# Layer 2's experts: results scattered to token order as they come, in place of a gather at the end

## The chip, the cores and the metric

One NeuronCore of a Trainium2 chip runs the whole program: TensorE (matmuls; the trace calls it PE, and PEld its weight loads), VectorE (DVE), ScalarE (ACT), GpSimd (POOL) and SyncE (SP, which issues plain DMAs). The metric is the time of one execution on the device in microseconds; less is better. The time of a kernel is the median of several runs.

## The reference

The program is a chain of four layers, each a mixer and a feed-forward part on 4096 tokens of 128 numbers. The change touches the feed-forward part of layer 2 alone, a mixture of eight experts with one expert per token and a capacity:

```python
def _route(tokens, router_w):
    capacity = int(math.ceil(T / E * CAPACITY_FACTOR))      # T 4096, E 8: 640
    probs = jax.nn.softmax(tokens @ router_w.T, axis=-1)
    top1_idx = jnp.argmax(probs, axis=-1)
    top1_prob = jnp.max(probs, axis=-1)
    order = jnp.lexsort((-top1_prob, top1_idx))
...
    pos_in_group = jnp.arange(T) - start[sorted_e]
    keep = jnp.zeros((T,), bool).at[order].set(pos_in_group < capacity)
    return jnp.where(keep, top1_idx, 0).astype(jnp.int32)

final_e = _route(tokens, router_w)
for e in range(E):
    h = jax.nn.relu(tokens @ W1[e] + b1[e])
    y = h @ W2[e] + b2[e]
    out = out + jnp.where((final_e == e)[:, None], y, 0.0)
```

`tokens` is the layer norm of the running state `x`, and `out` is added to `x`. A token that finds its expert full goes to expert 0.

## The kernel before

A token is one row of 128 numbers. In SBUF token `i * 128 + p` lies on partition `p` as tile `i` (32 tiles, `X` the state, `XN` its norm, `XT` the norm turned so that the features lie on the partitions). Layer 2's experts are `moe_capacity`, in three pieces, each a stage or a block with a barrier of all engines at its end (lines 60 to 64, and the block's own).

The first is a block of its own in which POOL clears `zero` (line 2010). The next is `capacity_route`: norm, turning, logits, softmax, and then the rank of each token inside its expert, found with 32 rounds of comparisons on VectorE and counting matmuls. In it ScalarE copies the turned groups out (`norm.take`, line 125) and then waits for VectorE's shifted logits, of which it takes the exponential (line 1921). SP loads the weights and writes seven blocks of zeros to DRAM in `prefetch`. Its result is `idx`, for each token the row of a DRAM tensor: rows 0 to 4479 are seven buckets of 640 rows for experts 1 to 7, and rows from 4480 on are the 4096 tokens in order, for those of expert 0.

In the last stage, `experts`, the work is cut into 22 units. Units 0 to 7 (the direct units) are expert 0 applied to all tokens from `XT`, 512 each, needing no routing. Units 8 to 21 are experts 1 to 7 in two parts each, 3 tiles and 2 tiles of 128 rows. A unit runs over TensorE (up, down, and turning back), ScalarE (ReLU and bias) and VectorE, which copies the result from PSUM to one of four buffers `yo` (line 2149). The order is written out by hand for each engine.

DMAs around it: POOL scatters the 32 tiles of `XN` to `xs_dram` by `idx`, one indirect DMA a tile (line 2033), beside the direct units. SP stores each unit's `yo` to `ys_dram` (line 2051) and loads the buckets of experts 1 to 7 (line 2045), the first two after unit 6's store. When all 22 stores have landed, POOL gathers from `ys_dram` by `idx`, again one indirect DMA a tile (line 2038), and VectorE adds the rows to `X`, a group of four tiles at a time (line 2162).

## Time and profile before

| | us |
|---|---|
| median of 3 runs | 3671.94 (3671.51 to 3673.9) |
| the profiled execution, time on the device | 3670.11 |
| the profiled execution, span from first to last instruction | 3668.4 |
| stretch that the change touches, clearing to last addition | 2150.8 to 2517.4 |
| of it: direct units | about 2296 to 2380 |
| of it: experts 1 to 7 | about 2380 to 2473 |
| of it: gathers and additions | about 2473 to 2517 |

A row of the timeline gives the start in us from the span's start, the time in us, the engine, the line of the kernel, the operation, what it writes and reads, and in square brackets how long the engine had been idle and what ended that. A row of the groups gives the count behind an x, then the busy time in us and the mean in ns. DMA-issuing instructions don't count as busy on SP, but the indirect ones on POOL do. "experts_", "route_" and "cap_" ahead of a name are the stage it belongs to.

### The profile page before, as it was taken

The numbers are of one execution on the slowest core, as the hardware profiler recorded it, in microseconds if no ns is written. First come the engines' busy times: TensorE is split into PE (matmuls) and PEld (weight loads), VectorE is DVE, ScalarE is ACT, GpSimd is POOL, SyncE is SP. The second block draws the span as 40 slices with busy tenths as digits, with TensorE's granted clock in tenths as the row PEclk, the third lists the DMA queues.
The fourth block names the chain that finished last, engine by engine and source line by source line (L and its number), as shares of the span: only waits on it lengthen the run. The fifth ranks groups of instructions, "written<-read, shape, count | busy, mean of one in ns | idle before, by whom it ended". The sixth has DMA issues, their size and how long they took to land. (4 is left out here: it accounts for less than half of the span.)

```text
span 3668.4 us, 31380 instructions
## 1 busy us (share of the span) xinstructions
PE 2677.9 (73%) x8896; PEld 1455.9 (40%) x8904; DVE 2129.6 (58%) x3695; ACT 1420.2 (39%) x3926; POOL 951.0 (26%) x620
## 2 busy tenths in 40 slices
PE   2007888999999889999877766782687787377317
PEld 1003344555555544444344442351344443255303
DVE  7997531222222366565534458013999996678686
ACT  1004333111111156666543320231798898233003
POOL 0003565000000000000122210303899999000005
PEclk6558999999999989999878879896887787689557
DMA  2001112000000074545200020112000000000001
GB/s 51 0 0 47 47 48 62 0 0 0 0 0 0 13 148 139 147 138 143 74 1 1 1 72 1 50 46 69 1 1 1 1 1 1 23 1 1 2 0 29
DMA packets 106429, 124.40 MB, mean 34 GB/s; under 512 B 21771, under 2 KB 59788, under 8 KB 106028
## 3 DMA queue, kind: packets, MB, share of 16 engines
q1 hardware_dynamic: 104236, 118.56, 12.2%
q0 software_dynamic: 2048, 4.20, 0.4%
q8 instruction: 55, 0.90, 0.1%
q14 instruction: 90, 0.74, 0.1%
HBM read 108.55 MB, written 14.16 MB: 33 GB/s over the span
## 5 line engine op out<-in xcount | busy, mean ns | idle before, releaser
L2325 POOL TENSOR_TENSOR dots_pr<-dots_g 128x1536 f32<-128x1536 f32 (+3 forms) x118 | 356.5, 3063 | 66.6 <-DVE dots_g L2450 54.0
L1012 DVE SCALAR_TENSOR_TENSOR attn_sim<-attn_sc,attn_mask 128x512 f32<-128x512 f32 (+3 forms) x256 | 125.8, 491 | 316.9 <-PE attn_sc L938 313.8
L938 PE MATMUL attn_sc<-attn_q,attn_xb 128*128 128x512 f32 (+3 forms) x768 | 295.0, 486 | 0.0
L949 PE MATMUL attn_op<-attn_sim,attn_v 128*128 128x512 f32 (+3 forms) x768 | 295.0, 486 | 0.0
L1298 DVE TENSOR_TENSOR grp_h<-grp_sq,grp_cb 128x512 f32<-128x512 f32 x256 | 176.5, 692 | 191.9 <-ACT grp_sq L1186 171.8
L1126 PE MATMUL grp_po<-grp_h,grp_down 128*128 128x512 f32 x512 | 266.4, 602 | 5.7 <-DVE grp_h L1298 5.7
L1118 PE MATMUL grp_ph<-all_xt,grp_up 128*128 128x512 f32 x512 | 264.0, 598 | 0.5 <-ACT grp_sg L1202 0.5
L2338 PE MATMUL dots_pu<-delta_wE,all_xt 128*128 128x264 f32 x512 | 193.3, 524 | 97.0 <-DVE dots_g L2450 95.6
L1180 ACT ACTIVATE grp_r<-grp_ph 128x512 f32<-128x512 f32 x272 | 162.4, 597 | 185.6 <-PE grp_ph L1118 183.9
L626 POOL TENSOR_TENSOR mix_h<-mix_r,mix_cb 128x512 f32<-128x512 f32 x128 | 179.4, 1413 | 123.8 <-ACT mix_r L540 90.3
L2392 ACT ACTIVATE dots_pr<-dots_pr 128x128 f32<-128x128 f32 x704 | 206.2, 300 | 3.5 <-POOL dots_pr L2325 3.5
L938 PEld LDWEIGHTS attn_sc<-attn_q,attn_xb 128*128 128x128 f32 x768 | 141.0, 190 | 125.7 <-issue 107.1
L2338 PEld LDWEIGHTS dots_pu<-delta_wE,all_xt 128*128 128x128 f32 x512 | 118.6, 249 | 175.8 <-DVE dots_g L2450 148.9
L2325 POOL TENSOR_TENSOR all_xn<-dots_g 128x1536 f32<-128x1536 f32 (+3 forms) x58 | 180.1, 3137 | 3.3 <-PE dots_fold L2348 3.3
L949 PEld LDWEIGHTS attn_op<-attn_sim,attn_v 128*128 128x128 f32 x768 | 141.0, 190 | 98.4 <-issue 68.9
L2447 DVE TENSOR_TENSOR dots_m<-dots_pu,dots_sg 128x512 f32<-128x512 f32 x256 | 164.7, 685 | 24.7 <-ACT dots_sg L2373 14.4
L2348 PE MATMUL dots_fold<-dots_pr,all_ident 128*128 128x512 f32 x336 | 160.0, 632 | 25.3 <-ACT dots_pr L2379 25.3
L378 PE MATMUL mix_po<-mix_woT,mix_y 128*128 128x128 f32 x128 | 17.1, 298 | 213.7 <-DVE mix_y L738 213.7
L2450 DVE SCALAR_TENSOR_TENSOR dots_g<-dots_m,dots_pu 128x512 f32<-128x512 f32 x256 | 163.3, 679 | 0.0
L1186 ACT ACTIVATE grp_sq<-grp_r 128x512 f32<-128x512 f32 x256 | 159.1, 621 | 0.0
L987 ACT ACTIVATE attn_sim<-attn_sc 128x512 f32<-128x512 f32 x128 | 76.4, 597 | 205.6 <-PE attn_sc L938 205.6
L1126 PEld LDWEIGHTS grp_po<-grp_h,grp_down 128*128 128x128 f32 x512 | 94.4, 191 | 138.8 <-issue 95.9
(612 smaller groups left out, 5341.5 us busy)
## 6 DMA issues: line engine op xcount, KB each, us to landing
grp_cb<-grp_combine SPq DMA_DIRECT2D x512, 128.0 KB, 3.2
mix_cb<-top_weights SPq DMA_DIRECT2D x64, 256.0 KB, 3.2
cap_xs<-cap_zero SPq DMA_DIRECT2D x7, 320.0 KB, 4.6
experts_xe<-cap_xs SPq DMA_DIRECT2D x7, 320.0 KB, 3.3
all_x<-in_L_attn_x_dram SPq DMA_DIRECT2D x4, 512.0 KB, 5.4
cap_w<-in_L_ffn_W_dram SPq DMA_DIRECT2D x1, 2048.0 KB
cap_ys<-experts_yo SPq DMA_DIRECT2D x8, 256.0 KB, 2.3
delta_h<-all_xn SPq DMA_DIRECT2D x1, 2048.0 KB
```

Of the source, the lines that this page charges most:

```text
L626: nc.gpsimd.tensor_tensor(h[:, J % HB], r[:, J % RB], cb[:, n % CB], ALU.mult).then_inc(h_ready, 1)
L938: nc.tensor.matmul(sc[k % SC][:, 0:w], xb[:, m * P:(m + 1) * P], q[:, par, n0:n0 + w], start=True, stop=True).then_inc(s_mm, 1)
L949: ins = nc.tensor.matmul(op[half][:, n0 - half * GROUP:n0 - half * GROUP + w], v[:, par, m], sim[:, par, k, 0:w], start=False, stop=False)
L1118: nc.tensor.matmul(ph[J % 2][:], w, XT[:, g * GROUP:(g + 1) * GROUP], start=True, stop=True).then_inc(up_mm, 1)
L1126: nc.tensor.matmul(po[g % 2][:], w, h[:, J % HB], start=(j == 0), stop=(j == NJ - 1)).then_inc(down_mm, 1)
L1180: nc.scalar.activation(r[:, J % RB], ph[J % 2][:], ACT.Relu).then_inc(relu_done, 1)
L1298: tt(h[:, J % HB], sq[:, J % RB], cb[:, n % CB], ALU.mult).then_inc(h_done, 1)
L2325: nc.gpsimd.tensor_tensor(dst, a, key, ALU.mult).then_inc(pp_ready, 1)
L2338: ins = nc.tensor.matmul(heads(n % PB)[:, q * HQ:(q + 1) * HQ], XTj[:, k // 2, j], wE[:, 1 - k % 2, h0:h0 + HQ], start=True, stop=True)
L2392: ins = nc.scalar.activation(v_, v_, ACT.Relu, accum_out=dots[:, 8 + r, j, h0:h0 + 1])
L2447: tt(m[:, sh], x[..., sh + 1:sh + 1 + D_], sg[:, n % PB], ALU.mult).then_inc(m_ready, 1)
L2450: ins = stt(g[:, I % 2, k, :, sh * D_:(sh + 1) * D_], m[:, sh], 0.0, x[..., 0:D_], ALU.max, ALU.mult)
```

## The change

Each row that is scattered to a bucket now carries a 129th number, the number of its token. The tile `rows` holds the norm's 128 numbers, copied by ScalarE, and the number, written by VectorE. Bucket rows which no token takes are filled beforehand with zeros and with numbers from 4096 up, so that they name rows behind the tokens. The direct units store their results to `y_dram` in token order. From each bucket VectorE takes the numbers (`place`), and POOL scatters each unit's results of experts 1 to 7 to the token's row of `y_dram`, one indirect DMA a tile (35 in all), as the results come. At the end SP loads `y_dram` in eight plain DMAs.

```diff
@@ capacity_route
@@ scalar
                 for g in range(NG):
                     norm.take(act, g)
+                act.wait_ge(norm.xn_ready, NT)
+                for g in range(NG):
+                    nc.scalar.activation(rows[:, g * TPG:(g + 1) * TPG, 0:C], XN[:, g * TPG:(g + 1) * TPG], ACT.Copy).then_inc(rows_ready, 1)
                 act.wait_ge(shifted, 1)
                 nc.scalar.activation(ex[:], lg[:], ACT.Exp).then_inc(exp_ready, 1)
...
@@ vector
                 dve.wait_ge(made, 3 + E)
+                c.link(nc.vector.tensor_copy(own[:].rearrange("p t a -> p (t a)"), number[:]))
+                c.link(ts(rows[:, :, C:C + 1], own[:], -1.0 * (E - 1) * capacity, None, ALU.add))
                 for i in range(NT):
...
-                c.link(nc.vector.tensor_copy(own[:].rearrange("p t a -> p (t a)"), number[:]))
                 c.link(tt(red[:], red[:], own[:], ALU.subtract))
@@ moe_capacity
-    xs_dram = nc.dram_tensor("cap_xs", [ROWS + T, C], F32).ap()
-    ys_dram = nc.dram_tensor("cap_ys", [ROWS + T, C], F32).ap()
+    xs_dram = nc.dram_tensor("cap_xs", [ROWS + T, C + 1], F32).ap()
+    y_dram = nc.dram_tensor("cap_y", [T + ROWS, C], F32).ap()
...
-        zero = s.sb("zero", [P, TPE, C])
+        zero = s.sb("zero", [P, (E - 1) * TPE, C + 1])
+        unused = s.sb("unused", [P, (E - 1) * TPE], mybir.dt.int32)
+        rows = s.sb("rows", [P, NT, C + 1])
...
-            sp.wait_ge(zeroed, 1)
-            for e in range(1, E):
-                sp.dma_start(xs_dram[(e - 1) * CAP:e * CAP].rearrange("(a p) c -> p a c", p=P), zero[:]).then_inc(cleared, 16)
+            sp.wait_ge(zeroed, 3)
+            sp.dma_start(xs_dram[0:ROWS].rearrange("(a p) c -> p a c", p=P), zero[:]).then_inc(cleared, 16)
...
                 nc.gpsimd.memset(zero[:], 0.0).then_inc(zeroed, 1)
+                nc.gpsimd.iota(unused[:], pattern=[[P, (E - 1) * TPE]], base=T, channel_multiplier=1).then_inc(zeroed, 1)
+                pool.wait_ge(zeroed, 2)
+                nc.gpsimd.tensor_copy(zero[:, :, C], unused[:]).then_inc(zeroed, 1)
...
@@ experts, gpsimd
                     for i in range(NT):
-                        nc.gpsimd.indirect_dma_start(xs_dram, bass.IndirectOffsetOnAxis(ap=idx[:, i:i + 1], axis=0), XN[:, i], None).then_inc(sent, 16)
+                        nc.gpsimd.indirect_dma_start(xs_dram, bass.IndirectOffsetOnAxis(ap=idx[:, i:i + 1], axis=0), rows[:, i], None).then_inc(sent, 16)
                     pool.wait_ge(sent, 16 * NT)
-                    for k in range(4):
-                        pool.wait_ge(stored[k], 16 * n_stored[k])
-                    for i in range(NT):
-                        nc.gpsimd.indirect_dma_start(XN[:, i], None, ys_dram, bass.IndirectOffsetOnAxis(ap=idx[:, i:i + 1], axis=0)).then_inc(back_in[i // TPG], 16)
+                    for U in range(ND - 4, ND):
+                        wait_stored(pool, U)
+                    for U in range(ND, NU):
+                        e, a, n = UNITS[U]
+                        pool.wait_ge(place_ready, e)
+                        pool.wait_ge(yo_ready, U + 1)
+                        for t in range(n):
+                            nc.gpsimd.indirect_dma_start(y_dram, bass.IndirectOffsetOnAxis(ap=place[:, e - 1, a + t:a + t + 1], axis=0),
+                                                         yo[:, U % 4, t], None).then_inc(put[U % 4], 16)
@@ experts, sync
-                    for U in range(ND, NU):
-                        if (U - ND) % 2 == 0 and UNITS[U][0] >= 2 and UNITS[U][0] + 1 < E:
-                            load(UNITS[U][0] + 1)
-                        store(U)
+                    for e in range(3, E):
+                        load(e)
+                    for U in range(NU - 4, NU):
+                        wait_stored(sp, U)
+                    for g in range(NG):
+                        r0 = g * GROUP
+                        sp.dma_start(XN[:, g * TPG:(g + 1) * TPG], y_dram[r0:r0 + GROUP].rearrange("(a p) c -> p a c", p=P)).then_inc(back_in[g], 16)
@@ experts, vector
+                        if a == 0:
+                            nc.vector.tensor_copy(place[:, e - 1], xe[:, e % 2, :, C]).then_inc(place_ready, 1)
                         nc.vector.tensor_copy(xeT[:, U % 2, 0:n * P], xt[U % 2][:, 0:n * P]).then_inc(xT_copied, 1)
...
                         if U >= 4:
-                            dve.wait_ge(stored[U % 4], 16 * (U // 4))
+                            wait_stored(dve, U - 4)
```

What stands in a row on each engine, before and now. First POOL, from the block ahead of the route on (`cap_zero` is the tile of zeros, `cap_unused` the numbers of the spare rows); a branch ends a block. Before:

```order
L2010 MEMSET cap_zero 128x640
L2006 UNCONDITIONAL_BRANCH
L1867 UNCONDITIONAL_BRANCH
L1869 MEMSET route_before 128x128
L1870 IOTA route_number 128x32
```

Now:

```order
L2017 MEMSET cap_zero 128x4515
L2018 IOTA cap_unused 128x35
L2020 CAST cap_zero<-cap_unused 128x35
L2013 UNCONDITIONAL_BRANCH
L1868 UNCONDITIONAL_BRANCH
L1870 MEMSET route_before 128x128
L1871 IOTA route_number 128x32
```

The memset is seven times as long, and two instructions stand behind it in the same block. Next ScalarE in the route, from the root of the variance to the probabilities' copies (`route_ex` is the exponential). Before:

```order
L113 ACTIVATE route_ln_dev<-route_ln_var,route_ln_eps 128x32
L125 ACTIVATE all_xt<-route_bank 128x512 x8
L1921 ACT_TABLE_LOAD
L1921 ACTIVATE route_ex<-route_lg 128x256
L1924 ACTIVATE route_pb<-route_bank 128x512 x8
```

Now:

```order
L113 ACTIVATE route_ln_dev<-route_ln_var,route_ln_eps 128x32
L125 ACTIVATE all_xt<-route_bank 128x512 x8
L1923 ACTIVATE cap_rows<-all_xn 128x4x128 x8
L1925 ACT_TABLE_LOAD
L1925 ACTIVATE route_ex<-route_lg 128x256
```

Eight copies stand ahead of the table load and the exponential. Last SP in the experts' stage, behind the stores of units 0 to 6 (`experts_yo` a unit's result, `experts_xe` a bucket). Before, with five more pairs of stores and five loads in all to the end:

```order
L2045 DMA experts_xe<-cap_xs 128x5x128 x2
L2051 DMA cap_ys<-experts_yo 128x4x128
L2051 DMA cap_ys<-experts_yo 128x3x128
L2051 DMA cap_ys<-experts_yo 128x2x128
L2045 DMA experts_xe<-cap_xs 128x5x128
```

Now, to the end of the stage:

```order
L2076 DMA cap_y<-experts_yo 128x4x128 x7
L2070 DMA experts_xe<-cap_xs 128x5x129 x2
L2076 DMA cap_y<-experts_yo 128x4x128
L2070 DMA experts_xe<-cap_xs 128x5x129 x5
L2090 DMA all_xn<-cap_y 128x4x128 x8
```

The stores between the loads are gone from SP, and the eight loads of the results stand at its end.

And POOL in the same stage, its whole list there. Before:

```order
L63 ISA
L2029 UNCONDITIONAL_BRANCH
L2033 DMA cap_xs<-all_xn,cap_idx 8576x128 x32
L2038 DMA all_xn<-cap_ys,cap_idx 128x128 x32
L2027 UNCONDITIONAL_BRANCH
```

Now:

```order
L63 ISA
L2048 UNCONDITIONAL_BRANCH
L2052 DMA cap_xs<-cap_rows,cap_idx 8576x129 x32
L2061 DMA cap_y<-experts_yo,experts_place 8576x128 x35
L2046 UNCONDITIONAL_BRANCH
```

The 32 gathers are gone, and 35 scatters of results stand in their place.

## Rows read from the trace of the kernel before

**Rows 1.** Windows of us: length, busy PE, PEld, DVE, ACT, POOL, clock, DMA, GB/s.

```profile
2296.00:2318.00 22.00, 22.00 (x51) 9.31 (x52) 0.69 (x1) 8.24 (x12) 16.60 (x17) 0.91 0.19 61
2380.00:2473.00 93.00, 79.45 (x300) 48.23 (x298) 14.45 (x29) 37.28 (x71) 0.00 (x0) 0.98 0.19 54
2473.00:2518.00 45.00, 0.00 (x0) 0.00 (x0) 5.61 (x8) 0.00 (x0) 30.22 (x32) 0.51 0.19 50
```

**Rows 2.** Timeline, the block ahead of the route and the route's first instructions.

```profile
2150.78 0.63 POOL L2010 MEMSET cap_zero<- 128x640 f32 x1 [19.33 <-POOLq L64]
2151.72 0.28 SPq L1864 DMA_DIRECT2D route_rw<-in_L_ffn_router_w_dram  x1
...
2151.80 0.06 DVE L92 MEMSET route_ln_eps<- 128x1 f32 x1 [2.32 <-PEq L2006]
```

**Rows 3.** Groups by form on POOL.

```profile
L2010 POOL MEMSET cap_zero<- 128x640 f32 x1 | 0.6, 631 | 19.3 <-POOLq L64 19.3
...
L1426 POOL MEMSET ssm_own<- 128x512 f32 x1 | 0.5, 524 | 0.0
...
L1870 POOL IOTA route_number<- 128x32 int32 x1 | 0.2, 163 | 0.0
```

**Rows 4.** Timeline, ScalarE and VectorE around the exponential.

```profile
2179.01 1.28 ACT L1921 ACT_TABLE_LOAD   x1
...
2182.53 0.42 DVE L1938 TENSOR_TENSOR route_lg<-route_lg,route_red 128x256 f32<-128x256 f32 x1
2182.99 0.42 ACT L1921 ACTIVATE route_ex<-route_lg 128x256 f32<-128x256 f32 x1 [2.69 <-DVE route_lg L1938]
```

**Rows 5.** Groups by form on ScalarE, a 128x512 from SBUF to SBUF.

```profile
L1186 ACT ACTIVATE grp_sq<-grp_r 128x512 f32<-128x512 f32 x256 | 159.1, 621 | 0.0
```

**Rows 6.** Timeline, two steps of VectorE's chain at the route's end.

```profile
2293.61 0.18 DVE L1967 CAST route_own<-route_number 128x32 f32<-128x32 int32 x1
2293.83 0.19 DVE L1968 TENSOR_TENSOR route_red<-route_red,route_own 128x32 f32<-128x32 f32 x1
```

**Rows 7.** POOL's scatters and gathers: ns min/median/max, first and last start.

```profile
L2033 POOL DMA_INDIRECT cap_xs<-all_xn,cap_idx x32: 954/958/1304, 2296.5 to 2336.0; - x32
...
L2038 POOL DMA_INDIRECT all_xn<-cap_ys,cap_idx x32: 940/944/984, 2475.4 to 2514.1; - x32
```

**Rows 8.** Timeline, the direct units: VectorE's copies, TensorE's wait, POOL's last scatter.

```profile
2310.89 0.69 DVE L2149 COPY experts_yo<-experts_bk 128x512 f32<-128x512 f32 x1 [16.20 <-PE experts_bk L2100]
2333.17 0.69 DVE L2149 COPY experts_yo<-experts_bk 128x512 f32<-128x512 f32 x1 [21.59 <-issue]
...
2335.99 0.96 POOL L2033 DMA_INDIRECT cap_xs<-all_xn,cap_idx  x1 [0.30 <-issue]
...
2342.35 1.22 PE L2090 MATMUL experts_dn<-experts_h,cap_w 128*128 128x512 f32 x1 [13.92 <-ACT experts_h L2128]
...
2349.12 0.69 DVE L2149 COPY experts_yo<-experts_bk 128x512 f32<-128x512 f32 x1 [15.26 <-PE experts_bk L2100]
2356.61 0.69 DVE L2149 COPY experts_yo<-experts_bk 128x512 f32<-128x512 f32 x1 [6.80 <-PE experts_bk L2100]
```

**Rows 9.** Timeline, the first loads of buckets and TensorE's wait for them.

```profile
2380.21 1.13 SPq L2045 DMA_DIRECT2D experts_xe<-cap_xs  x2
...
2383.77 0.55 PE L2073 MATMUL experts_xt<-all_ident,experts_xe 128*128 128x128 f32 x3 [3.00 <-DMA experts_xe<-cap_xs]
```

**Rows 10.** Timeline, from the last copies out of PSUM to the last addition.

```profile
2470.36 0.56 DVE L2149 COPY experts_yo<-experts_bk 128x384 f32<-128x384 f32 x1 [3.68 <-PE experts_bk L2100]
...
2472.30 0.42 DVE L2149 COPY experts_yo<-experts_bk 128x256 f32<-128x256 f32 x1 [1.38 <-PE experts_bk L2100]
2475.42 0.98 POOL L2038 DMA_INDIRECT all_xn<-cap_ys,cap_idx  x1 [138.47 <-DMA cap_ys<-experts_yo]
...
2514.15 0.94 POOL L2038 DMA_INDIRECT all_xn<-cap_ys,cap_idx  x1 [0.30 <-issue]
2516.66 0.69 DVE L2162 TENSOR_TENSOR all_x<-all_xn,all_x 128x512 f32<-128x512 f32 x1 [4.25 <-DMA all_xn<-cap_ys,cap_idx]
```

**Rows 11.** Windows, five us in which the queues load weights, columns as in rows 1.

```profile
2163.00:2168.00 5.00, 5.00 (x26) 4.87 (x25) 5.00 (x21) 1.42 (x3) 0.00 (x0) 0.50 1.05 305
```

More of the change, by code:

```diff
@@ L1834, in _, with capacity_route @@
                 dve.wait_ge(x_added, 2 * BATCH)
-def capacity_route(nc, X, XN, XT, ident, router_w, idx, capacity, prefetch):
+def capacity_route(nc, X, XN, XT, ident, router_w, idx, rows, capacity, prefetch):
     E = router_w.shape[0]
@@ L1858, in capacity_route @@
             "ahead_ready", "cnt_mm", "cnt_ready", "cntT_mm", "vector_chain"))
+        rows_ready = s.sem("rows_ready")
         norm = Norm(nc, s, X, XN, XT, ident, bank[2:4])
@@ L1928, in _ @@
                 act.wait_ge(cnt_ready, NG)
+                act.wait_ge(rows_ready, NG)
             @block.vector
@@ L2010, in _ @@
                 nc.gpsimd.memset(zero[:], 0.0).then_inc(zeroed, 1)
-        capacity_route(nc, X, XN, XT, ident, router_w, idx, CAP, prefetch)
+                nc.gpsimd.iota(unused[:], pattern=[[P, (E - 1) * TPE]], base=T, channel_multiplier=1).then_inc(zeroed, 1)
+                pool.wait_ge(zeroed, 2)
+                nc.gpsimd.tensor_copy(zero[:, :, C], unused[:]).then_inc(zeroed, 1)
+        capacity_route(nc, X, XN, XT, ident, router_w, idx, rows, CAP, prefetch)
         with Stage(nc, "experts") as s1:
-            xe = s1.sb("xe", [P, 2, TPE, C])
+            xe = s1.sb("xe", [P, 2, TPE, C + 1])
+            place = s1.sb("place", [P, E - 1, TPE], U32)
             xeT = s1.sb("xeT", [P, 2, GROUP])
@@ L2024, in moe_capacity, with wait_stored @@
             back_in = [s1.sem(f"back_in{g}") for g in range(NG)]
-            n_stored = [sum(1 for U in range(NU) if U % 4 == k) for k in range(4)]
+            place_ready = s1.sem("place_ready")
+            put = [s1.sem(f"put{k}") for k in range(4)]
+            def wait_stored(eng, U):
+                if U < ND:
+                    eng.wait_ge(stored[U % 4], 16 * (U // 4 + 1))
+                else:
+                    eng.wait_ge(put[U % 4], 16 * sum(n for V, (e, a, n) in enumerate(UNITS[:U + 1]) if V >= ND and V % 4 == U % 4))
             with nc.Block() as block:
@@ L2030, in _ @@
                 def _(pool):
[L2031 removed]
+                    pool.wait_ge(cleared, 16)
                     for i in range(NT):
[L2033 removed]
+                        nc.gpsimd.indirect_dma_start(xs_dram, bass.IndirectOffsetOnAxis(ap=idx[:, i:i + 1], axis=0), rows[:, i], None).then_inc(sent, 16)
                     pool.wait_ge(sent, 16 * NT)
[L2035 to L2038 removed]
+                    for U in range(ND - 4, ND):
[7 more added lines that the diff above has]
+                                                         yo[:, U % 4, t], None).then_inc(put[U % 4], 16)
                 @block.sync
@@ L2044, in load @@
                             sp.wait_ge(x_mm, 2 * (e - 2))
+                            sp.wait_ge(place_ready, e - 2)
                         sp.dma_start(xe[:, e % 2], xs_dram[(e - 1) * CAP:e * CAP].rearrange("(a p) c -> p a c", p=P)).then_inc(xe_in[e - 1], 16)
@@ L2048, in store @@
                         e, a, n = UNITS[U]
-                        r0 = (ROWS if e == 0 else (e - 1) * CAP) + a * P
+                        r0 = a * P
                         sp.wait_ge(yo_ready, U + 1)
-                        sp.dma_start(ys_dram[r0:r0 + n * P].rearrange("(a p) c -> p a c", p=P), yo[:, U % 4, 0:n]).then_inc(stored[U % 4], 16)
+                        sp.dma_start(y_dram[r0:r0 + n * P].rearrange("(a p) c -> p a c", p=P), yo[:, U % 4, 0:n]).then_inc(stored[U % 4], 16)
                     for U in range(ND - 1):
@@ L2072, in turn_in @@
                         for t in range(n):
-                            ins = nc.tensor.transpose(xt[U % 2][:, t * P:(t + 1) * P], xe[:, e % 2, a + t], ident[:])
+                            ins = nc.tensor.transpose(xt[U % 2][:, t * P:(t + 1) * P], xe[:, e % 2, a + t, 0:C], ident[:])
                         ins.then_inc(x_mm, 1)
@@ L2159, in _ @@
                     for g in range(NG):
-                        dve.wait_ge(back_in[g], 16 * TPG)
+                        dve.wait_ge(back_in[g], 16)
                         xt_ = X[:, g * TPG:(g + 1) * TPG]
```

1 line of the change is left out of this document (removed).

## The prediction

> **What bounds the kernel now.** I read the views in this order: the windows by stage, the timeline around layer 2's experts, the groups by form for the price of single instructions, and the timeline of each engine where one waits long. All of the change lies in one part of the span, from the end of layer 2's mixer to the start of layer 3, about 370 of 3668.4 us. In the windows [rows 1] the stage of experts 1 to 7 (2380 to 2473) is TensorE's: 79.45 of 93 us busy at a granted clock of 0.98. The 45 us behind it are nobody's: TensorE and ScalarE do nothing, VectorE 5.61 us, and POOL issues 32 gathers. The timeline [rows 10] shows the chain there: the last result leaves PSUM at 2472.72 (2472.30 + 0.42), SP stores it, POOL's first gather starts at 2475.42, its last at 2514.15, and VectorE's last addition runs from 2516.66 to 2517.35. The 32 are 0.94 us each and stand (2514.1 - 2475.4) / 31 = 1.25 us apart [rows 7]. The tail is 2517.35 - 2472.72 = 44.6 us long. This is what the change goes for.
>
> A second idle stretch matters for the rivals. In the stage of the direct units VectorE copies out at 2310.89, 2333.17, 2349.12 and 2356.61 [rows 8]. The last two are 7.49 us apart. From 2310.89 to 2349.12 two units took 38.23 us in place of 14.98: 23.2 us are lost there, TensorE idle for 13.92 us before 2342.35, and it ends soon after POOL's last scatter (started 2335.99). For VectorE's wait of 21.59 us before 2333.17 the view names "issue", no engine. That scatters run at that time and at no other time of the before kernel beside matmuls is all the trace has.
>
> **The change part by part.**
>
> 1. *The tail goes, a shorter one comes.* Removed: the store of the last unit, 32 gathers, the landing: 44.6 us. In its place: unit 20's result (3 tiles) is out at 2470.92, unit 21's (2 tiles) at 2472.72 [rows 10]. The trace has the same form of instruction for the new scatters, the 32 of line 2033, 0.96 us long and (2336.0 - 2296.5) / 31 = 1.27 us apart [rows 7]. POOL starts the five at 2471.0, 2472.3, 2473.5, 2474.8 and 2476.0. How long one takes to land no row shows; from below it is the 1.0 us of its own issue, from above the 2.5 us of a gather (2514.15 to 2516.66 [rows 10]), and I take 2.5, the nearest row: 2478.5. Then eight plain loads of 256 KB. The first load of a kind that moves rows of 512 bytes needed 3.56 us (2380.21 to 2383.77 [rows 9]) for 320 KB. Where such transfers are back to back the queues moved 305 GB/s [rows 11], while the queues were full; 2.1 MB are 7.0 us at that rate, and 10 us at 210 GB/s, which is 320 KB in 3.56 less 2 us, where 2 us stands for what a transfer takes whatever its size, a little under a gather's 2.5. So the last load lands 2 + 7 to 2 + 10 us after 2478.6; I take 10, nearer the full queues, since eight are in a row: 2488.6. Seven of the eight additions (0.7 us) hide under the next load's 1.1 us, one does not: 2489.3. The new tail is 16.6 us (bounds 14 to 19). **Gain 28.0 us.**
>
> 2. *POOL's work in the block ahead of the route.* The block holds nothing but POOL's clearing, and all engines wait for its end: SP's first load stands at 2151.72 and VectorE's first work at 2151.80, right behind the memset from 2150.78 to 2151.41 [rows 2]. So each ns here is on the path. A memset of 512 elements takes 524 ns, of 640 elements 631 ns [rows 3], 0.84 ns an element; 4515 elements are 0.63 + 3875 x 0.00084 = 3.88 us, 3.25 more than now. The added iota is 0.16 us [rows 3]. The cast of 35 numbers onto a strided row has the iota on 32 as its nearest row; I bound it by 0.1 and 0.3 us and take 0.2, with 0.1 for the wait ahead of it. **Cost 3.7 us** (3.4 to 4.2).
>
> 3. *Eight copies on ScalarE.* They stand between its last take and the exponential. Now the table load fills that gap, 2179.01 to 2180.29, and the exponential starts at 2182.99, just behind VectorE's subtraction [rows 4]. A copy of 128x512 from SBUF to SBUF is 0.62 us [rows 5], and back to back they overlap a little, so eight are 4.3 to 5.0 us: 2183.6 at the middle, and then the table load, 1.28 us, which the order puts behind them: 2184.9. The exponential starts 1.9 us late (1.5 to 2.4), and VectorE's chain hangs on it. **Cost 1.9 us**; the first 4 us of the copies are covered by the logits' matmuls and VectorE's three steps.
>
> 4. *VectorE's number in each row.* One more chained step, and the cast is moved ahead: steps of the chain are 0.22 us apart [rows 6]. **Cost 0.2 us.** In the experts' stage seven casts of 5 numbers each stand before the copy that TensorE waits for; up to 0.18 us [rows 6], at least 0.06 [rows 2]: 7 x 0.13. **Cost 0.9 us.**
>
> 5. *Rows of 516 bytes.* Each first scatter and each load of a bucket moves 129 numbers. POOL's issue should stay at 1.27 us; up to twice that is hidden, since the scatters end at 2337 and SP asks for them only at 2380.21 [rows 8, 9], 43 us later. Of the loads one is on the path, the first: TensorE waits 3.00 us for it [rows 9]. **Cost 0.3 us** (0 to 1.5). The loads of experts 3 to 7 are issued when a buffer is free, a whole expert (12.7 us) ahead of use, against 3.56 us.
>
> 6. *Moved without a price.* SP no longer stores the 14 units of experts 1 to 7; only the last of these was waited for, and it is in term 1. POOL's 35 scatters run beside TensorE: five for each expert are 5 x 1.27 = 6.3 us, and an expert takes (2472.72 - 2383.77) / 7 = 12.7 us [rows 9, 10]. If POOL fell behind, VectorE would wait before a fourth unit's copy, 24 us later. The zero fill, one DMA for seven, is queued behind the weights as before and is wanted only by the first scatter at 2296.5 [rows 7].
>
> Sum: -28.0 + 3.7 + 1.9 + 0.2 + 0.9 + 0.3 = -21.0 us. The profiled execution took 3670.1 us, 1.8 below the median 3671.9, with the same tail as any; from the median the forecast is **3651 us**, 0.57% less.
>
> The Trainium skill, "SBUF — State Buffer", section "Who interferes with whom", says that a DMA never contends with a compute engine, and that a DMA issued from POOL can itself be held back by certain VectorE copies. By it the new scatters cost TensorE nothing, and the sum stays 3651. The trace does not bear it out fully: the 23.2 us of [rows 8] fall beside such DMAs, while POOL's scatters keep their 1.27 us apart across VectorE's copies at 2310.89 and 2333.17 [rows 7, 8]. So I give the next rival a chance that this rule alone would not.
>
> **The rivals.**
>
> *Scatters stop TensorE* (the slower side). If what happened from 2318 to 2341 comes from POOL's indirect DMAs, it can come again from 2397 on, where 35 of them now run beside matmuls. For it: the stretch stands in that stage alone, and ends some 4 us behind the last scatter. Against it: 17 of the 32 scatters ran before 2318 beside a TensorE that was busy 22.00 of 22 us [rows 1], and the new ones come in groups of two and three with pauses. They wait for TensorE's results too, so a stop drains POOL and ends itself. At worst TensorE stands while POOL issues: 35 x 1.27 = 44 us, so 3651 + 44 = **3695**. It decides from 21 us on, about half of that. A weaker return, 14 to 28 us, gives 3665 to 3679: no difference that can be told.
>
> *The old stop goes.* The first 32 scatters change too (another source, 4 bytes more a row). If the stop hangs on such detail it may vanish: 3651 - 23 = **3628**.
>
> *Long rows are dear.* If a row of 516 bytes made a scatter three times as long, they would end at 2296.5 + 32 x 3.8 = 2418, 38 us after SP needs them: **3689**. Nothing in the trace has such rows. Up to (2380 - 2296.5) / 32 = 2.6 us each it costs nothing.
>
> *The change doesn't do what it says.* The order excludes it: POOL's list has no gather any more.
>
> **How the numbers follow.** Forecast 0.57 (its own range 3645 to 3657, from the bounds of the terms); old stop gone or much shorter 0.12; stops return at 14 to 28 us 0.14; stops return in full 0.12; long rows 0.05. About 0.2% (7 us) is what a measurement of this kernel can tell from no change. Faster: 0.57 + 0.12 = 0.69. Same: 0.14. Slower: 0.17. The range takes in the vanished stop and the weak return up to the old time: 3626 to 3674, and leaves out 0.05 + 0.12 and a little above and below.
>
> **What would show it.** Right: from the last copy out of PSUM to the last addition some 16.6 us; POOL's memset near 3.9 us with VectorE's statistics 3.7 us later behind the mixer; a table load behind eight copies, and the exponential 1.9 us later against the statistics; copies out in the direct stage with the same gap of 23 us; experts 1 to 7 in 90 us. Wrong: a unit of experts 1 to 7 with TensorE idle for more than a few us while POOL scatters; the gap in the direct stage gone; POOL's scatters more than 2.6 us apart; the eight loads slower than 1.5 us each.

## The result, and the profile after

| | us |
|---|---|
| before, median of 4 runs | 3671.73 (3671.41 to 3673.90) |
| changed kernel, median of 4 runs | 3644.30 (3641.51 to 3650.35) |
| ratio | 0.9926, 95% interval 0.9913 to 0.9938 |
| profiled execution of the changed kernel, span | 3639.8 |

The change makes the kernel 0.74% faster: 27.4 us, with 23 to 32 by the interval. The prediction said 21.0.

The mixer ahead ended 1.01 us later in this execution (2150.49, before 2149.48), so I compare lengths, not places. The timeline of the changed kernel, the block ahead of the route:

```profile
2151.80 3.86 POOL L2017 MEMSET cap_zero<- 128x4515 f32 x1 [19.32 <-POOLq L64]
2155.61 0.17 POOL L2018 IOTA cap_unused<- 128x35 int32 x1
2155.86 0.24 POOL L2020 CAST cap_zero<-cap_unused 128x35 f32<-128x35 int32 x1
2156.40 0.28 SPq L1865 DMA_DIRECT2D route_rw<-in_L_ffn_router_w_dram  x1
...
2156.48 0.06 DVE L92 MEMSET route_ln_eps<- 128x1 f32 x1 [5.99 <-PEq L2013]
```

VectorE waited 5.99 us here in place of 2.32 [rows 2], 3.67 more. The timeline around the exponential:

```profile
2183.58 4.25 ACT L1923 ACTIVATE cap_rows<-all_xn 128x512 f32<-128x512 f32 x8
...
2187.21 0.42 DVE L1943 TENSOR_TENSOR route_lg<-route_lg,route_red 128x256 f32<-128x256 f32 x1
2187.85 1.28 ACT L1925 ACT_TABLE_LOAD   x1
2189.14 0.42 ACT L1925 ACTIVATE route_ex<-route_lg 128x256 f32<-128x256 f32 x1
```

The exponential starts 1.51 us behind the end of the subtraction (2187.63), where before it was 0.04 us [rows 4]. The copies are done at 2187.83, 0.20 us behind the subtraction, so nearly all that VectorE waits for is the table load.

The direct units and POOL's scatters beside them. First VectorE's copies out, then the line of the scatters (ns min/median/max, first and last start):

```profile
2318.42 0.69 DVE L2179 COPY experts_yo<-experts_bk 128x512 f32<-128x512 f32 x1 [16.50 <-PE experts_bk L2128]
2341.02 0.69 DVE L2179 COPY experts_yo<-experts_bk 128x512 f32<-128x512 f32 x1 [21.90 <-remote]
2356.60 0.69 DVE L2179 COPY experts_yo<-experts_bk 128x512 f32<-128x512 f32 x1 [14.89 <-PE experts_bk L2128]
```

```profile
L2052 POOL DMA_INDIRECT cap_xs<-cap_rows,cap_idx x32: 954/958/1304, 2303.8 to 2343.3; - x32
```

Two units took 38.18 us, before 38.23 [rows 8]: the stop of 23 us is there again, to 0.05 us. Rows of 516 bytes leave the scatters 1.27 us apart, as in [rows 7].

The stage of experts 1 to 7 and the tail, in windows (columns as in rows 1), and the line of the result scatters:

```profile
2388.00:2481.00 93.00, 78.93 (x299) 48.21 (x298) 14.95 (x36) 37.29 (x71) 29.81 (x32) 0.98 0.18 52
2481.00:2498.00 17.00, 0.00 (x0) 0.00 (x0) 5.54 (x8) 0.00 (x0) 3.69 (x4) 0.52 0.52 143
```

```profile
L2061 POOL DMA_INDIRECT cap_y<-experts_yo,experts_place x35: 952/957/961, 2405.7 to 2484.6; - x35
```

TensorE is busy 78.93 of 93 us with POOL now busy 29.81 beside it, before 79.45 with POOL idle [rows 1]. The stretch behind it in which TensorE does nothing is 17 us long in place of 45. The timeline of the tail:

```profile
2480.22 0.42 DVE L2179 COPY experts_yo<-experts_bk 128x256 f32<-128x256 f32 x1 [1.38 <-PE experts_bk L2128]
2490.01 1.53 DVE L2192 TENSOR_TENSOR all_x<-all_xn,all_x 128x512 f32<-128x512 f32 x2 [9.37 <-DMA all_xn<-cap_y]
...
2495.38 2.19 DVE L2192 TENSOR_TENSOR all_x<-all_xn,all_x 128x512 f32<-128x512 f32 x3 [0.21 <-DMA all_xn<-cap_y]
2499.09 4.16 SPq L2249 DMA_DIRECT2D wload_wn<-in_L_attn_W_qkvb_dram  x6
```

From the last copy out (2480.64) to the end of the last addition (2497.57) are 16.93 us, where 44.63 us stood [rows 10]. Then layer 3's first load comes 1.52 us later. In the kernel before it came 4.34 us behind the last addition; its row there is:

```profile
2521.69 4.31 SPq L2219 DMA_DIRECT2D wload_wn<-in_L_attn_W_qkvb_dram  x6
```

That is a gain of 2.8 us that I had not foreseen. Up to the start of layer 3 the profiled executions differ by 23.6 us. The spans differ by 28.6 us; a mixer 1.0 us longer makes that 29.6 to explain, so from the start of layer 3 on 6.0 us more were gained, where the change edits nothing.

### The profile page after: what moved, and what is told of

Same layout as the page of the kernel before. It is cut to its first block and busy times, and to the rows that moved or that the text cites. A ratio compares the mean times of both kernels' runs of the same rounds, so it can differ in the third digit from the quotient of the medians.

```text
span 3639.8 us, 31419 instructions
## 1 busy us (share of the span) xinstructions
PE 2681.1 (74%) x8904; PEld 1456.0 (40%) x8904; DVE 2130.4 (59%) x3703; ACT 1424.6 (39%) x3934; POOL 958.4 (26%) x625
```

## The experiments

There were eleven runs in three series, each series on one chip with its own runs of the kernel before. The theory they test: the sum of the prediction holds, term for term; the extra 2.8 us at the stage's end belong to POOL's indirect DMAs; the rest of the extra gain is chance in layer 3. The rivals: layer 3 gains with the changed kernel; the scatters of results cost TensorE something; the old stop is called up by some detail of the kernels.

This table is worked out from the timelines of all profiles, lengths in us. "clear": from the mixer's end to VectorE's statistics. "exp": from the subtraction's end to the exponential. "u0 to u6": from the copy out of unit 0 to that of unit 6, the direct units. "u6 to u7": between those copies, with the wait for the first bucket. "experts": from the copy of unit 7 to the end of the last copy. "tail": to the end of the last addition. "end": to layer 3's statistics. "all": from the mixer's end to there.

| kernel | clear | exp | u0 to u6 | u6 to u7 | experts | tail | end | all |
|---|---|---|---|---|---|---|---|---|
| before (prediction) | 2.32 | 0.03 | 68.20 | 12.18 | 81.45 | 44.63 | 4.39 | 372.3 |
| after (result) | 5.99 | 1.50 | 68.15 | 12.21 | 81.87 | 16.92 | 1.61 | 348.7 |
| e5 before again | 2.32 | 0.03 | 44.96 | 13.49 | 81.47 | 45.28 | 4.33 | 351.5 |
| e6 after again | 5.99 | 1.51 | 44.96 | 12.12 | 81.90 | 16.79 | 1.61 | 325.3 |
| e1 additions only | 6.00 | 1.51 | 44.96 | 12.22 | 81.90 | 44.66 | 4.46 | 356.1 |
| e4 spaced | 5.99 | 1.51 | 44.96 | 12.16 | 81.90 | 16.68 | 1.61 | 325.3 |
| e3 scatters late | 5.99 | 1.51 | 44.96 | 32.37 | 81.90 | 17.25 | 1.61 | 346.0 |
| e9 scatter last | 5.99 | 1.51 | 44.96 | 12.14 | 81.90 | 17.03 | 7.84 | 331.8 |
| e2 moved | 1.38 | 0.03 | 44.96 | 13.66 | 81.90 | 16.71 | 1.61 | 320.4 |
| e7 loads early | 1.38 | 0.03 | 44.96 | 7.64 | 81.90 | 16.56 | 1.61 | 314.2 |
| e8 two queues | 1.38 | 0.03 | 44.96 | 7.64 | 81.90 | 17.05 | 1.61 | 314.7 |

**e1_additions_only: all that is added, without the shorter tail.** The changed kernel, with the gathers, the stores and the loads' order of the kernel before.

```diff
-                    for U in range(ND, NU):
-                        ...
-                            nc.gpsimd.indirect_dma_start(y_dram, ... place[:, e - 1, a + t:a + t + 1] ..., yo[:, U % 4, t], None)
+                    for i in range(NT):
+                        nc.gpsimd.indirect_dma_start(XN[:, i], None, ys_dram, ... idx[:, i:i + 1] ...).then_inc(back_in[i // TPG], 16)
```

> The changed kernel with the end of the experts' stage as it was: SP stores all units, POOL gathers at the end. All that the change adds ahead of the results stays (larger clearing, ScalarE's copies, the number in each row, rows of 129, the casts to place). Theory (the sum): the additions cost about 7 us, so 3671.7 + 7 = 3678.7 us, and the tail from the last copy out of PSUM to the last addition is 44.6 us again; then POOL's last gather starts 3.2 us before the last addition ends and the next stage starts some 4.3 us after that addition, because the end of POOL's block comes 6.3 us after the start of its last indirect DMA. Rival (layer 3 itself is 6 us faster in the changed kernel, as its one profile shows, for a reason that lies in the additions): 3673 us or less.

Measured: 3657.98 us against 3650.62, ratio 1.0022 (1.0013 to 1.0032), a cost of 7.4 us, between 4.7 and 11.7 by the interval. The sum had said 7.0, and the rival (3673 us or less beside 3671.7, so hardly a cost) falls. That the two numbers are so near is in part luck: by the table "all" is 4.6 us longer than in e5, and from the start of layer 3 to the span's end this profile has 1149.5 us where e5 has 1147.1. The tail is 44.66 us long. Its end in the timeline:

```profile
2498.20 0.94 POOL L2051 DMA_INDIRECT all_xn<-cap_ys,cap_idx  x1 [0.30 <-issue]
2500.65 0.69 DVE L2178 TENSOR_TENSOR all_x<-all_xn,all_x 128x512 f32<-128x512 f32 x1 [4.10 <-DMA all_xn<-cap_ys,cap_idx]
...
2505.74 4.31 SPq L2235 DMA_DIRECT2D wload_wn<-in_L_attn_W_qkvb_dram  x6
```

The next stage begins 7.54 us behind the start of the last gather. In the kernel before it is the same number, 2521.69 - 2514.15 = 7.54 [rows 10]. What I had not expected was the level: before took 3650.6 us here, 21 us less than in the first comparison, and the direct units stood at 7.49 us each, with no stop.

**e5_before_again and e6_after_again: both kernels unchanged, on another chip.**

> The kernel before, unchanged. In the runs so far the stop of 23 us in the direct units stood in the profiles of before and after taken together with the prediction, and in none of the four profiles of the next series, though two of these leave the scatters as they are; before took 3671.7 us there and 3650.6 here. Theory (the stop belongs to the chip or its condition, not to the kernel): either 3650 us and copies 7.5 us apart, or 3671 us and the gap of 38 us, and e6 shows the same as this one. Rival (some detail of the kernels called it up): this profile has the gap and e6 or e7 does not, or the other way round.

> The changed kernel, unchanged. The sum of its parts as its first profile shows them is a gain of 23.6 us up to the start of layer 3 (tail 27.7 us shorter, end of POOL's block 2.8, additions -6.9), the other 4 to 5 us of the first comparison lie in layer 3, which the change does not touch. Theory (layer 3 differs by chance): 3650.6 - 23.6 = 3627 us, ratio 0.9935. Rival (layer 3 gains): 3650.6 - 28 = 3622.6 us, ratio 0.9923.

Measured: e5 3652.37 us (one run), with these copies in its timeline:

```profile
2314.01 0.69 DVE L2149 COPY experts_yo<-experts_bk 128x512 f32<-128x512 f32 x1 [15.71 <-PE experts_bk L2100]
2321.50 0.69 DVE L2149 COPY experts_yo<-experts_bk 128x512 f32<-128x512 f32 x1 [6.80 <-PE experts_bk L2100]
2328.99 0.69 DVE L2149 COPY experts_yo<-experts_bk 128x512 f32<-128x512 f32 x1 [6.80 <-PE experts_bk L2100]
```

The kernel of [rows 8], word for word, with 7.49 us between copies. e6: 3625.70 us (3621.81 to 3626.89) against 3649.39, ratio 0.9936 (0.9923 to 0.9950), with no stop either. So the stop was there with both kernels in the first comparison, and with none of the kernels in the three later series. It doesn't depend on which of the two kernels runs, and its 23 us cancel in the comparison. The gain without it is 23.7 us by the medians, where theory and rival had said 23.6 and 28. Its interval reaches from 18 to 28 us and overlaps that of the first comparison (0.9913 to 0.9938, 0.9923 to 0.9950), so the medians alone don't decide between the two.

Where the first comparison's further us came from, windows of layer 3's output stage show (columns as in rows 1). Each goes from the start of the stage's first product on VectorE to the end of its last addition there: before, e5, after, e6.

```profile
3198.22:3404.32 206.10, 158.81 (x891) 121.58 (x890) 156.25 (x160) 69.50 (x126) 0.00 (x0) 0.89 0.00 1
```

```profile
3179.85:3386.46 206.61, 159.35 (x892) 121.73 (x890) 156.20 (x160) 69.53 (x126) 0.00 (x0) 0.89 0.00 1
```

```profile
3175.61:3376.14 200.53, 158.29 (x891) 120.26 (x890) 156.24 (x160) 69.53 (x126) 0.00 (x0) 0.91 0.00 1
```

```profile
3155.93:3356.48 200.55, 158.31 (x891) 120.29 (x890) 156.22 (x160) 69.50 (x126) 0.00 (x0) 0.91 0.00 1
```

The same work takes 200.5 to 200.6 us in the profiles of after and e6, and of e3 and e11 below, and 206.0 to 206.6 us in the nine others: before, e5, and e1, e2, e4 and e7 to e10, which carry the same additions. So it is not a product of the additions as such. But chance, as my theory had it, isn't shown either. Four kernels have two profiles each, taken in different series (before with e5, after with e6, e3 with e11, e7 with e10), and each fell twice on the same side. By that these 5.6 us go with the kernel as it was built, and the changed kernel has them both times. What sets the side is open. Other parts behind the experts differ by 2 to 3 us even between two profiles of one kernel: from the start of layer 3 to the span's end they take 1140.6 us in after, 1143.5 in e6, and up to 1149.7 in e4. The profile of e6 was the fastest of its five runs, 3.9 us under their median.

**e4_scatters_spaced: the first scatters in groups of five.**

```diff
                     for i in range(NT):
+                        if i % 5 == 0 and i:
+                            pool.wait_ge(yo_ready, i // 5)
                         nc.gpsimd.indirect_dma_start(xs_dram, ...
```

> The changed kernel, POOL's scatters in groups of five, the next group when one more direct unit's result is out, so that each group (6.3 us) is followed by a pause of about 1 us and the 32 scatters reach over six units. If the stop needs an unbroken row of scatters: it is gone, 3644.3 - 23 = 3621 us. If the number of scatters beside direct units is what matters: a stop of some length remains, between 3621 and 3644. If scatters have nothing to do with it: 3644 and the same gap of 38 us between the copies of units 0 and 2.

Measured: 3628.03 us, ratio 0.9938 (0.9921 to 0.9954), the same as the changed kernel's 0.9936. The direct units take 44.96 us, no stop. But e1 and e2 of the same series, with their scatters in one row, have no stop either, so this run doesn't tell what it was made for. It shows that spacing costs nothing: the scatters still end well ahead of the first load of a bucket.

**e3_scatters_late and e11_scatters_late: the first scatter behind unit 3's result.**

```diff
                     for i in range(NT):
+                        if i == 0:
+                            pool.wait_ge(yo_ready, 4)
                         nc.gpsimd.indirect_dma_start(xs_dram, ...
```

> The changed kernel, POOL's first scatter waits until unit 3's result is out. The question is the stop of 23 us in the direct units. If continuous scatters cause it: no gap of VectorE's copies in units 0 to 3 (7.5 us apart), and a gap beginning some 15 to 22 us behind the first scatter, lasting until about 4 us after the last. If it belongs to the start of the stage (the first stores, the weights, code): the gap between the copies of units 0 and 2 is 38 us as before, with no scatter running. The time is near 3644 in both cases, since the first bucket's load waits for the last scatter.

> The same kernel as e3: the changed kernel, POOL's first scatter waits for unit 3's result. It tells something new only where the stop of 23 us is present, which is seen in the time of the runs of before (3671 us) and in e10. There: if the scatters carry the stop, it moves behind the first scatter; if not, it stays between the copies of units 0 and 2, with no scatter running. Without the stop it repeats e3: 3642 us, copies 7.5 us apart.

Measured: 3642.05 and 3644.69 us (one run each), no gap anywhere in the direct units. Without the stop they say only what late scatters cost. TensorE's row ahead of the first bucket in e3:

```profile
2388.45 0.90 PE L2103 MATMUL experts_xt<-all_ident,experts_xe 128*128 128x128 f32 x3 [22.67 <-DMA experts_xe<-cap_xs]
```

It waits 22.67 us for scatters of which POOL issues the last until 2383.7. By the table the late start costs 20.7 us of "all" (346.0 against 325.3 in e6), while the small delays of e4 cost nothing.

**e9_scatter_last: one more indirect DMA at the end.** POOL repeats its last scatter when the last load has landed.

```diff
+                    pool.wait_ge(back_in[NG - 1], 16)
+                    nc.gpsimd.indirect_dma_start(y_dram, ... place[:, E - 2, TPE - 1:TPE] ..., yo[:, (NU - 1) % 4, 1], None).then_inc(extra, 16)
...
                     dve.wait_ge(x_added, NG)
+                    dve.wait_ge(extra, 16)
```

> The changed kernel with one more indirect DMA: when the last of the eight final loads has landed, POOL repeats its last scatter (same rows, same values), and VectorE waits for its landing behind the additions. It prices the end of POOL's block. Theory (the block ends 6.3 us after the start of POOL's last indirect DMA, as at the end of before and of e1, whatever the landing): the next stage's first load stands 6.3 + 1.3 = 7.6 us behind the start of that scatter. Rival (only the landing counts, 2.5 us as that of a gather): 2.5 + 1.5 = 4.0 us behind it.

Measured, from its timeline:

```profile
2470.28 2.16 DVE L2194 TENSOR_TENSOR all_x<-all_xn,all_x 128x512 f32<-128x512 f32 x3 [0.21 <-DMA all_xn<-cap_y]
2471.99 1.28 POOL L2064 DMA_INDIRECT cap_y<-experts_yo,experts_place  x1 [11.62 <-DMA all_xn<-cap_y]
2480.20 4.18 SPq L2252 DMA_DIRECT2D wload_wn<-in_L_attn_W_qkvb_dram  x6
```

Layer 3 starts 8.21 us behind the start of that scatter (the scatter itself took 1.28 in place of 0.96 us), near the theory's 7.6 and far from the rival's 4.0. The "end" column goes from 1.61 to 7.84 us. The view of the DMAs issued from 2471 to 2481 gives the landing of the added scatter, in us from its issue:

```profile
cap_y<-experts_yo,experts_place POOLq DMA_INDIRECT x1, 2.5
```

So it wasn't the landing that the stage waited for. The traces hold one instruction more, POOL's DRAIN, which stands behind its last indirect DMA and ahead of its signal to the others. It ends 6.24 to 6.25 us behind the start of the last gather in before, e5 and e1, 6.91 us behind that of the added scatter in e9, and 6.5 us behind that of the last scatter in after, e6 and e7. In after that is 2491.15, 6.4 us ahead of the end of the last addition, so there it costs nothing. An indirect DMA of POOL thus holds the end of its stage for some 7.5 us from its start, longer than its data need: in e1 VectorE could use the last gather's data 2.45 us after its start.

**e2_moved: clearing inside the route, copies of rows behind the probabilities' copies.**

```diff
-        with nc.Block() as block:
-            @block.gpsimd
-            def _(pool):
-                nc.gpsimd.memset(zero[:], 0.0).then_inc(zeroed, 1)
-                ...
@@ capacity_route, gpsimd
                 nc.gpsimd.affine_select(out=before[:], ...).then_inc(made, 1)
+                clear(pool)
@@ capacity_route, scalar
                     nc.scalar.activation(pb[:, ...], bank[2 + g % 2][:], ACT.Copy).then_inc(pb_ready, 1)
+                act.wait_ge(norm.xn_ready, NT)
+                for g in range(NG):
+                    nc.scalar.activation(rows[:, g * TPG:(g + 1) * TPG, 0:C], XN[:, g * TPG:(g + 1) * TPG], ACT.Copy).then_inc(rows_ready, 1)
```

> The changed kernel with two of its parts placed elsewhere: POOL clears inside the route's block, behind its own small memsets, so the block ahead of the route is gone; and ScalarE's eight copies of rows stand behind the probabilities' copies, ahead of the counts, where ScalarE waits about 90 us. Theory (both lie on the path where they stand): the route's first load starts 4.6 us earlier against the end of the mixer (3.9 + 0.4 us of POOL's work and the block's barrier), the exponential 1.5 us earlier behind the subtraction, together -6.1, so 3644.3 - 6.1 = 3638 us. Rival (something else is late next, the zero fill or the copies ahead of the first scatter): the first scatter does not start earlier, and the time stays at 3644.

Measured: 3617.20 us, ratio 0.9909 (0.9893 to 0.9926). In its timeline:

```profile
2150.22 0.20 POOL L1870 MEMSET route_before<- 128x128 f32 x1 [19.32 <-POOLq L64]
2150.29 0.06 DVE L92 MEMSET route_ln_eps<- 128x1 f32 x1 [1.38 <-PEq L64]
...
2151.14 3.86 POOL L2015 MEMSET cap_zero<- 128x4515 f32 x1
...
2181.48 0.42 ACT L1923 ACTIVATE route_ex<-route_lg 128x256 f32<-128x256 f32 x1 [2.69 <-DVE route_lg L1944]
...
2189.77 4.26 ACT L1929 ACTIVATE cap_rows<-all_xn 128x512 f32<-128x512 f32 x8
```

The same memset of 3.86 us now costs nothing, and the copies run in ScalarE's long wait. VectorE's wait fell from 5.99 to 1.38 us, the exponential follows the subtraction at once: -4.61 and -1.48 us, as expected. Of this 1.5 us came back behind the wait for the first bucket ("u6 to u7" 13.66), so that "all" is 4.9 us shorter. e5 has 13.49 there with the kernel before, so this part doesn't hang on the move; e7 shows what it is. The medians say more: 10.8 us under e4 of the same series (3628.03), whose "all" is that of the changed kernel. The profiles have the other part from the start of layer 3 on, 1145.4 us in e2 and 1149.7 in e4, where the moves edit nothing; it isn't put down to them.

**e7_loads_early and e10_loads_early: the first two buckets loaded behind unit 4's store.** The two are one kernel.

```diff
-                    for U in range(ND - 1):
+                    for U in range(5):
                         store(U)
                     sp.wait_ge(sent, 16 * NT)
                     load(1)
                     load(2)
-                    store(ND - 1)
+                    for U in range(5, ND):
+                        store(U)
```

> e2 (clearing inside the route, copies of rows later) with one more move: SP loads the first two buckets behind the store of unit 4 in place of unit 6. Theory (TensorE's wait of 3 us and more ahead of unit 8 is there because SP stands at the store of unit 6, not for the scatters): the copies of units 6 and 7 are about 7.5 us apart instead of 13.7, the wait on TensorE ahead of the first turned bucket is under 0.5 us, and the stage ends 3.0 to 3.5 us earlier: 3614 us. Rival (the last scatter's landing is what counts): the wait stays.

> The same kernel as e7 (clearing inside the route, ScalarE's copies later, first two buckets loaded behind the store of unit 4), timed, since e8, which differs from it by the second queue only, gained nothing over it. By the traces: e6 23.7 us under before, e2's two moves 6.1 more, the early loads 3.3 more: 33 us under before, ratio 0.991. Where the stop of 23 us in the direct units is present (before at 3671 us in place of 3650), the early loads still help, since the scatters end during the stop; the ratio is the same.

Measured: e7 3613.02 us (one run), e10 3613.89 us against 3651.86, ratio 0.9895 (0.9879 to 0.9912), 38.0 us where I had expected 33. TensorE's first turned bucket, first in e2, then in e7:

```profile
2360.27 0.55 PE L2099 MATMUL experts_xt<-all_ident,experts_xe 128*128 128x128 f32 x3 [3.15 <-DMA experts_xe<-cap_xs]
```

```profile
2358.52 0.49 PE L2100 MATMUL experts_xt<-all_ident,experts_xe 128*128 128x128 f32 x3
```

and SP's loads, in the same order:

```profile
2356.56 1.13 SPq L2068 DMA_DIRECT2D experts_xe<-cap_xs  x2
```

```profile
2343.14 1.12 SPq L2068 DMA_DIRECT2D experts_xe<-cap_xs  x2
```

The wait of 3.15 us is gone; the copies of units 6 and 7 are 7.64 us apart, in the other builds with a wait 12.1 to 13.7. The wait for the first bucket [rows 9] was not for the scatters, it was for SP, which stood at unit 6's store with both loads behind it. The gain is more than my 3.3 us: 4.5 against the changed kernel (12.12 in e6) and 6.0 against e2. The windows behind the first turned bucket tell why, e2 in ten us and e7 in five:

```profile
2360.00:2365.00 5.00, 4.01 (x9) 2.21 (x10) 0.63 (x2) 1.08 (x2) 0.00 (x0) 0.57 0.10 28
2365.00:2370.00 5.00, 5.00 (x16) 2.94 (x15) 0.69 (x1) 1.24 (x3) 0.00 (x0) 0.75 0.01 3
```

```profile
2358.00:2363.00 5.00, 4.25 (x14) 2.13 (x13) 0.63 (x2) 1.94 (x4) 0.00 (x0) 1.00 0.18 56
```

After the idle 3.15 us TensorE ran at a granted clock of 0.57 and then 0.75 of 2.4 GHz, so in part at its lower level, 1.2 GHz; without the wait it stayed at 1.00. From the turning to unit 7's copy are 8.83 us in e2 and 6.12 in e7, 2.7 us for the clock beside 3.3 for the wait; TensorE's further wait in between is 0.72 us in both. The price is not always that high: in e6, with 2.99 us idle, the window behind the wait has 0.66 and the next 1.00, and the same stretch takes 7.44 us, 1.3 more than in e7. That is how 12.1 and 13.7 come about.

**e8_two_queues: the final loads from SP and ScalarE.** e7, with every second load issued by ScalarE.

```diff
-                    for g in range(NG):
+                    for g in range(0, NG, 2):
                         sp.dma_start(XN[:, g * TPG:(g + 1) * TPG], ...
@@ scalar
+                    for U in range(NU - 4, NU):
+                        wait_stored(act, U)
+                    for g in range(1, NG, 2):
+                        act.dma_start(XN[:, g * TPG:(g + 1) * TPG], ...
```

> e7 with the eight final loads issued from two engines, SP the even and ScalarE the odd ones. Theory (issuing bounds them: 5.7 us for eight on SP): the time from the first issue to the last addition falls from 10.6 to about 9 us, bounded then by 2.1 MB at some 300 GB/s, so 3612.5 us. Rival (the transfers bound them already): no change against e7. Against the kernel before the sum of all moves is -23.6 - 6.1 - 3.3 - 1.5 = -34.5 us.

Measured: 3614.40 us, ratio 0.9903 (0.9888 to 0.9918), no better than e7 and e10. Its timeline and a window of the five us in which the loads land:

```profile
2454.49 2.02 SPq L2089 DMA_DIRECT2D all_xn<-cap_y  x4
2454.50 2.12 ACTq L2165 DMA_DIRECT2D all_xn<-cap_y  x4
...
2463.92 1.29 DVE L2196 TENSOR_TENSOR all_x<-all_xn,all_x 128x512 f32<-128x512 f32 x2 [0.36 <-DMA all_xn<-cap_y]
```

```profile
2459.00:2464.00 5.00, 0.00 (x0) 0.00 (x0) 3.37 (x7) 0.00 (x0) 0.00 (x0) 0.50 1.04 251
```

All eight loads are issued in 2.1 us in place of 5.7, and the last addition still ends at 2465.21, 10.7 us behind the first issue (10.6 in the changed kernel: 2486.96 to 2497.57). The DMA share is 1.04: the queues are full. With one issuing engine they are full just as long: in e7 the three windows of two us from 2454.85 to 2460.85, from 2 to 8 us behind the first issue, have shares of 1.00, 1.14 and 1.19 at 280 to 316 GB/s. The rival holds, the transfers bound this part.

## Why the prediction was right, point by point

*The tail (term 1).* Predicted 16.6 us in place of 44.6, measured 16.93. The last scatter started at 2484.64, 4.0 us behind the last copy out, against 3.3 predicted, since POOL's group of five began 0.8 us behind unit 20's result; SP asked 2.3 us later (I took 2.5), and the loads took 10.6 us to the last addition, against 10.7. Gain 27.7, predicted 28.0.

*The block ahead of the route (term 2).* Predicted 3.7, measured 3.67; e2 shows that it was all on the path.

*ScalarE's copies (term 3).* Predicted 1.9, measured 1.47: eight copies took 4.25 us, the lower bound of my 4.3 to 5.0, where I had taken the middle. The size was off, the mechanism held, the table load included.

*VectorE's step and casts (term 4).* Predicted 0.2 and 0.9, measured 0.07 (from the exponential to the last step of the route 112.60 us, 112.53 in e5) and 0.42 ("experts" 81.87 against 81.45). The cast of five numbers takes 0.17 us but the next copy starts only 0.08 us later: the two overlap, and the term was half of what I took.

*Long rows (term 5).* Predicted 0.3, measured 0.03 in "u6 to u7", less than the clock makes of that part (12.1 to 13.7).

*What was missing.* The end of POOL's block, 2.8 us of gain. The prediction removed the 32 gathers up to the last landing and left the stage's end as it was. The row was there to be read: SP's next load at 2521.69 in the kernel before stands 4.34 us behind the last addition's end, where a stage's end elsewhere takes 1.5. The sum with this term is -23.8, and measured are -23.6 in the pair of profiles and -23.7 in the medians of e6. That these are so near is in part luck. The terms as measured add up to -24.8. In the first profile of before the route was by chance 1.0 us shorter than in all others, which hides as much, and the stretch from the route's last step to unit 0's copy, for which I had no term, took 16.50 us in place of 16.20 (15.71 in e5, 16.05 where the copies are moved). Between e5 and e6, the other pair, "all" is 26.2 us shorter: there the tails differ by 28.5 us, and "u6 to u7" is 1.4 us longer in e5.

*The rest of the -27.4* lies from layer 3 on, as far as the profiles tell: 200.5 us in place of 206.1 in its output stage, in both profiles of the changed kernel. Other parts there go up and down by 2 to 3 us, so that the medians of e6 show nothing of it. Why a kernel in which layer 3 is unchanged has the shorter stage is open, and the prediction had no term for it.

*The rivals.* "Scatters stop TensorE" fell: "experts" is 81.90 us in e6 with 35 scatters and 81.90 us in e1 with none. This also agrees with the rule of the Trainium skill, "SBUF — State Buffer", section "Who interferes with whom", as far as it says that a DMA doesn't contend with a compute engine. My doubt about it came from the stop. "Long rows are dear" fell: 0.958 us a scatter, as before. "The old stop goes" did happen in the later series, but to both kernels, so it was a wrong rival for the change: I took a stretch of one trace for a property of the kernel. What the stop is remains open. That it stood beside scatters says nothing, as the same scatters ran without it in the eleven later profiles, in eight of them in one row from the stage's start, and the kernels made to tell more (e3 with e11, and e4) never met it.

*The range.* 3626 to 3674 held the time, most of its width for a stop that cancels. My own range for the forecast, 3645 to 3657, was missed by 0.7 us; the missing term alone is more than that.

*Better than both.* e10, 3613.9 us, is 38.0 us under before (ratio 0.9895) and 14 us more than the changed kernel's gain of 23.7. The three moves put 4.6, 1.5 and 4.5 us of waiting away or under other work. By "all" they are 325.3 - 314.4 = 10.9 us (e10's is 314.4); the other 3 us are within the intervals. The 4.6 are more than the change had added there (3.7), since the block itself is gone.

## What to carry to other kernels

A stage's tail can be summed up from the nearest rows and came out within 0.4 us here, its parts off by up to 0.7 us and to both sides; but read also the gap between its last useful instruction and the next stage's first: an engine's own leftovers can stand there. Small preparation cost its full length here in a block of its own, and its overhang ahead of a step that a chained engine waited for, and nothing a few lines further on; look for the engine's longest wait and put it there. A load behind an unrelated wait in a queue's order is paid like a slow load, and here the clock was paid on top of TensorE's idle 3 us; moving it cost nothing. Before a stall becomes a rival, see it twice: take a second profile on another chip. And when the time moves where nothing was edited, profile both kernels twice before it is called chance.

## What the hardware showed that I had not expected

- A stage whose last work on POOL is an indirect DMA ends late: the next stage's first load stands 7.54 us behind that DMA's start (before, e1 and e5 alike; 8.21 in e9), though a gather's data can be used after 2.5 us. The Trainium skill, "Perfetto Trace Analysis", section "DMA Instruction — SWDGE (GPSIMD)", says that the profile's end of such an instruction is the end of making its descriptors, not the end of the transfer. The rows agree (0.94 us of issue, 2.5 us to use), and the 7.5 us are longer than either: POOL's DRAIN ends only 6.2 to 6.9 us behind that start.
- The stop: 23.2 us in the direct units with both kernels in the first comparison, to 0.05 us, and none in eleven profiles of three other series. Before took 3671.7 us with it and 3649 to 3652 us without.
- An idle stretch of 3.15 us on TensorE cost 2.7 us more behind it, at a granted clock of 0.57 and 0.75 in the next ten us (e2), where e7 without it has 1.00. One of 2.99 us in e6 cost 1.3.
- Layer 3's output stage took 200.5 or 206 us for the same instructions, and each kernel profiled twice fell twice on the same side.
- Eight loads of 256 KB from DRAM need 10.3 us from the first issue to the last addition when one engine issues them (e7: 2452.85 to 2463.10) and 10.7 us when two do (e8), with the queues full for six us of it at 280 to 317 GB/s.
